# Layer 3's attention rows spread over partitions by DMA through DRAM, and a new order of work between layers 2 and 3

## What is computed

```python
def _L3_gnn_ref(X, A, Wv, bv, aw, ab, Wk, bk):
    Xw = X @ Wv + bv
    sj = Xw @ aw[:d, 0]
    si = Xw @ aw[d:, 0]
    e = leaky_relu(sj[:, None, :] + si[:, :, None] + ab[0], negative_slope=0.2)
    alpha_matrix = A * exp(e)
    transition = alpha_matrix / (sum(alpha_matrix, axis=-1, keepdims=True) + 1e-12)
    H = 0; Xk = X
    for k in range(3):
        H = H + Xk @ Wk[k] + bk[k]
        Xk = einsum('bij,bjd->bid', transition, Xk)
    return relu(H)
```

## Time and profile before

| what | value |
|---|---|
| median of 3 runs | 2437.7 us (2436.69 to 2437.82) |
| the profiled execution's own time | 2437.03 us |
| its span in the profile | 2435.1 us |
| PE matmuls busy | 2363.6 us (97%) |
| DVE, ACT, POOL busy | 1335.6, 818.1, 846.5 us (55%, 34%, 35%) |
| PE's idle time by releaser, largest | 17.3 us in 15 waits at L586, 14.4 in 2 at L303, 8.0 in 1 at L313 |

### The profile page before, as it was taken

One profiled execution on the slowest core, in us unless ns is written; L12 is line 12 of the kernel. 1 busy time (PEld: TensorE's weight loads), 2 busy tenths in 40 slices (PEclk: granted clock), 3 DMA queues, 4 the chain that ended last, 5 costly groups with the idle time before them and its releaser, 6 DMA issues.

```text
span 2435.1 us, 39821 instructions
## 1 busy us (share of the span) xinstructions
PE 2363.6 (97%) x16095; PEld 1932.4 (79%) x16095; DVE 1335.6 (55%) x2572; ACT 818.1 (34%) x1493; POOL 846.5 (35%) x1040
## 2 busy tenths in 40 slices
PE   7899999999999999999999999999789999999998
PEld 4688888888888887888888888888678888887877
DVE  2566555566556544445544455444666666665653
ACT  2344343334333333333333333333322222323221
POOL 2355445445545423233322333222441313131221
PEclk9899999999999999999999999999899999999999
DMA  5222333232333333222322223112332222223221
GB/s 169 68 81 74 88 100 92 81 85 74 82 89 107 90 111 100 57 57 71 99 58 57 57 72 98 57 57 83 102 92 72 89 73 86 77 75 88 71 72 38
DMA packets 152057, 197.98 MB, mean 81 GB/s; under 512 B 61936, under 2 KB 62016, under 8 KB 151872
## 3 DMA queue, kind: packets, MB, share of 16 engines
q1 hardware_dynamic: 151872, 195.42, 28.1%
HBM read 77.90 MB, written 50.33 MB: 53 GB/s over the span
## 4 chain that ended last, share of the span: by engine, by line
PE 71%; DVE 7%; issue 7%; POOL 6%; SPq 5%; ACT 3%; DMA 1%; ACTq 0%; DVEq 0%; POOLq 0%
PE bank L313 31%; PE bank L303 28%; SPq L1441 5%; POOL h3T_lo L1221 3%; PE bank L329 3%; PE bank L375 2%; DVE hs L665 2%; DVE stA L644 2%; ACT hn L980 1%; PE bank L522 1%; PE bank L495 1%; PE bank L293 1%; PE bank L505 1%; DVE yt L939 1%; POOL stA L1211 1%
## 5 line engine op out<-in xcount | busy, mean ns | idle before, releaser
L313 PE MATMUL bank<-w_hi,h3T_hi 128*128 128x512 f32 x768 | 304.1, 396 | 0.0
L313 PE MATMUL bank<-w_hi,h3T_lo 128*128 128x512 f32 x768 | 299.5, 390 | 0.0
L313 PE MATMUL bank<-w_lo,h3T_hi 128*128 128x512 f32 x768 | 299.5, 390 | 0.0
L633 DVE TENSOR_TENSOR Z_lo<-bank,Z_hi 128x512 fp32r<-128x512 f32 x128 | 82.9, 685 | 216.9 <-ACT Z_hi L966 216.9
L980 ACT ACTIVATE hn<-x,stA 128x512 f32<-128x512 f32 x192 | 140.7, 804 | 145.1 <-POOL stA L1213 144.1
L1208 POOL TENSOR_SCALAR stA<-stA 128x4 f32<-128x4 f32 x48 | 11.6, 242 | 485.7 <-DVE stA L646 485.6
L313 PEld LDWEIGHTS bank<-w_hi,h3T_lo 128*128 128x128 f32 x768 | 144.4, 188 | 30.4
L313 PEld LDWEIGHTS bank<-w_lo,h3T_hi 128*128 128x128 f32 x768 | 144.7, 188 | 29.8
L313 PEld LDWEIGHTS bank<-w_hi,h3T_hi 128*128 128x128 f32 x768 | 144.8, 189 | 29.5
L665 DVE STREAM_TRANSPOSE hs<-hn 128x512 f32<-128x512 f32 x192 | 123.9, 688 | 74.1 <-ACT hn L980 74.1
L633 DVE TENSOR_TENSOR cT_lo<-bank,cT_hi 128x256 fp32r<-128x256 f32 x128 | 44.8, 411 | 206.2 <-ACT cT_hi L966 206.2
(11 more groups left out here) (246 smaller groups left out, 6165.6 us busy)
## 6 DMA issues: line engine op xcount, KB each, us to landing
hGA<-hs SPq DMA_DIRECT2D x768, 64.0 KB, 2.0
mid<-x SPq DMA_DIRECT2D x32, 1024.0 KB, 4.6
x<-mid SPq DMA_DIRECT2D x32, 1024.0 KB, 5.7
x<-in_x SPq DMA_DIRECT2D x16, 1024.0 KB, 6.0
hGB<-hs SPq DMA_DIRECT2D x256, 64.0 KB, 2.0
out<-x SPq DMA_DIRECT2D x16, 1024.0 KB, 4.9
abf<-in_adj SPq DMA_DIRECT2D x64, 64.0 KB, 5.1
adj<-in_adj SPq DMA_DIRECT2D x64, 64.0 KB, 3.3
```

What stands on the lines that cost most here:

```text
L313: ins = eng.matmul(b[:], h[l][:, k, ts], W[r][:, k, :], start=(k == 0 and i == 0), stop=(last and k == 3 and i == 2))
L633: return eng.tensor_tensor(lo, src, hi.bitcast(F), ALU.subtract)
```

## The change

1. The eight `abr` tiles, their matmuls and the copies out of the banks are gone. SP writes the columns `af` to DRAM (two DMAs of 512 single elements) and reads them back as `arow`, repeated over 128 partitions.
2. The `sib` tile, its four matmuls and its bank are gone. For each group SP writes the si column to DRAM (one DMA of 512 single elements), waits for it, and reads it back as `si`, one row on all partitions (`rows3`). This stands behind the group's gather and ahead of the store of the group before.
3. In layer 3 `l3_alpha` on DVE and ACT stands behind all four z1 evictions (before: behind the third); POOL's `features_lo` stands ahead of `l3_alpha` (before: behind it).
4. Where layer 2 passes to layer 3: DVE interleaves the sums of group 0 with the VV additions; PE does both contexts ahead of the first output product and transposes group 0's adjacency there; ACT splits W3[2] and copies group 0's features ahead of the second context; group 0's alpha is taken before layer 3's loop, its row sum after the first z2 product, Thi after the second (before: after the fourth); W3[2] is split by POOL one step later.

```diff
-        ones3, bones = alloc(pc, "ones3t", [128, 128]), alloc(pc, "bones", [128, 128])
-        abr = [alloc(pc, f"abr{i}", [128, 128]) for i in range(2)]
+        si = alloc(pc, "sirows", [128, 4, 128])
+        bones = alloc(pc, "bones", [128, 128])
...
# PE
-                if prev:
+                if on and prev:
                     l2_out(g - 1, 0)
                     l2_ctx(g - 1, 1)
+                elif prev:
+                    l2_ctx(g - 1, 1)
+                    l2_out(g - 1, 0)
+                    l3_adj(0)
...
-                if g == NG - 1:
-                    for h in range(2):
-                        b, full, before = bank.take(("arow", h), (v_arow, h + 1))
...
                 for t in range(4):
                     gemm(("z2", g, t), hT3[i], t, W3[2], (v_zlo[0], 4 * g + t + 1))
                     if g == 0 and t == 0:
-                        l3_alpha(0)
-                    if g == 0 and t == 3:
                         l3_rowsum(0)
...
                     if t == 2:
-                        l3_alpha(g + 1)
+                        l3_adj(g + 1)
...
# DVE
+            def l3_alpha(g):
+                dve.wait_ge(d_si, 16 * (g + 1))
+                dve.wait_ge(v_sc, g + 1)
+                for h in HALF:
+                    eng.tensor_tensor(zc[h, :, :], si[h, :, h], scol[g % 2][h, :, 0:1].to_broadcast([64, 4, 64]),
+                                      ALU.add).then_inc(v_zc, 1)
...
+                        if g == NG - 1 and t >= 1:
+                            l3_sums(dve, eng, 0, ((0,), (1,), (2, 3))[t - 1])
...
                 for t in range(4):
                     l3_zlo(1, ("z1", g, t), g, t)
-                    if t == 2:
-                        l3_alpha(g + 1)
+                l3_alpha(g + 1)
...
# ACT
+                if not on:
+                    split_in_place(W3[2], d_w2)
+                    act.wait_ge(v_cst, 1)
+                    features2_hi(3, 0, hT3[0])
...
# POOL
-                l3_rowsource(g + 1)
-                l3_alpha(g + 1)
                 if g + 1 < NG:
                     features_lo(3, g + 1, hT3[(g + 1) % 2], hGA, p_flo3)
+                l3_alpha(g + 1)
                 l3_rowsum(g + 1)
...
# SP
+            def rows3(g):
+                if g < NG:
+                    sp.wait_ge(v_sc, g + 1)
+                    eng.dma_start(si_dr[g].rearrange("(t p) -> p t", p=128), scol[g % 2][:, :, 1], allow_slow_non_contiguous=True).then_inc(d_sc, 16)
+                    sp.wait_ge(d_sc, 16 * (g + 1))
+                    sp.wait_ge(v_zc, 2 * g)
+                    sp.wait_ge(*bank.done(("pT", NG - 1, 3)))
+                    eng.dma_start(si[:].rearrange("p t n -> p (t n)"), si_dr[g].partition_broadcast(128)).then_inc(d_si, 16)
...
+                    sp.wait_ge(v_af, 8)
+                    for h in range(2):
+                        eng.dma_start(ar_dr[h].rearrange("(k p) -> p k", p=128), af[:, :, h], allow_slow_non_contiguous=True).then_inc(d_ac, 16)
+                    sp.wait_ge(d_ac, 32)
+                    eng.dma_start(arow[:].rearrange("p h d -> p (h d)"),
+                                  ar_dr.rearrange("h d -> (h d)").partition_broadcast(128)).then_inc(d_ar, 16)
...
                 load3(g + 2)
                 gather(3, g + 1)
+                rows3(g + 1)
                 sp.wait_ge(v_x4, 4 * g + 4)
                 store_x(kA(3, g), out_v[g])
```

More of the change, by code:

```diff
@@ L81, in build @@
            for i in range(2)]
+    si_dr = [nc.dram_tensor(f"si{g}", [GT], F, kind="Internal").ap() for g in range(NG)]
+    ar_dr = nc.dram_tensor("arows", [2, D], F, kind="Internal").ap()
     mask_v = nodemask.rearrange("(g t a) n -> g a t n", g=NG, t=4)
@@ L574, in pe_program @@
                         l2_pT(g, r)
[L577 to L587, removed]
             def l3_rowsum(g):
@@ L864, in dve_program @@
                     transposes(3, 0)
-                    for h in range(2):
-                        dve.wait_ge(*bank.done(("arow", h)))
-                        eng.tensor_copy(arow[:, h, :], bank.of(("arow", h))[:]).then_inc(v_arow, 1)
                     m = dve.step(eng.tensor_tensor(sc3[:], awb[:, 0, :], awb[:, 1, :], ALU.add))
@@ L945, in l3_sums @@
         def l3_sums(dve, eng, g, ts):
-            dve.wait_ge(v_arow, 2)
-            dve.wait_ge(p_sib, g - 1)
+            dve.wait_ge(d_ar, 16)
+            dve.wait_ge(d_sc, 16 * (g - 1))
+            if g == 0:
+                dve.wait_ge(*bank.done(("qk", NG - 1, 3)))
             for t in ts:
@@ L1110, in l2_exp, with l3_alpha @@
                     eng.activation(zt[r][:], zt[r][:], ACT.Exp, scale=0.25).then_inc(a_e2, 1)
+            def l3_alpha(g):
+                if g >= NG:
+                    return
+                act.wait_ge(p_al, g - 1)
+                adj_T(3, g)
+                act.wait_ge(v_lr, g + 1)
+                eng.activation(ec3[:], ec3[:], ACT.Exp).then_inc(a_ee, 1)
             for g in range(NG + 1):
@@ L1292, in l2_residual @@
                         eng.tensor_tensor(xt[:, t, :], xt[:, t, :], bo2[:], ALU.add).then_inc(p_xb, 1)
-            def l3_rows():
-                pool.wait_ge(v_af, 8)
-                for h in range(2):
-                    for k in range(4):
-                        i = 4 * h + k
-                        if i >= 2:
-                            if i == 5:
-                                pool.wait_ge(*bank.done(("arow", 0)))
-                            else:
-                                pool.wait_ge(s_pe, {2: 1, 3: 2, 4: 3, 6: 4, 7: 5}[i])
-                        eng.tensor_tensor(abr[k % 2][:], ones3[:], af[:, k, h:h + 1].to_broadcast([128, 128]), ALU.mult).then_inc(p_row, 1)
             l2_residual(0)
@@ L1330, in pool_program @@
                         scale_A(3, 0)
[L1331 removed]
+                if g == NG - 1:
+                    eng.memset(bones[:], 0.0).then_inc(p_bones, 1)
+                    pool.wait_ge(p_bones, 1)
+                    for h in HALF:
+                        eng.memset(bones[h, h], 1.0).then_inc(p_bones, 1)
+                    pool.wait_ge(p_bones, 3)
+                    pool.wait_ge(*bank.done(("qk", g, 3)))
+                    for tl in T:
+                        for n in ("hi", "lo"):
+                            eng.memset(tl[n][:].bitcast(F), 0.0).then_inc(p_zero3, 1)
                 if g == NG:
+                    split_in_place(W3[2], "w2")
                     features_lo(3, 0, hT3[0], hGA, p_flo3)
[L1334 to L1345 removed]
             def l3_alpha(g):
@@ L1547, in sp_program @@
                     load_adj3(1)
+                    rows3(0)
                 if prev:
```

97 lines of the change are left out of this document (26 added, 71 removed).

## The result

| what | before | changed kernel |
|---|---|---|
| median | 2437.76 us (4 runs) | **2551.69 us** (4 runs, 2549.95 to 2552.93) |
| ratio | | **1.0466**, 95% interval 1.0448 to 1.0484 |
| S of group 1 | 1794.67 | 1779.79 |
| S to S, mean of groups 2 to 15 | 41.24 | 49.94 |
| last S to the end of the span | 60.1 | 70.4 |

The kernel is 114 us slower, where 34 us faster was forecast. As in the prediction, S is the moment when SP has issued a group's 16 gather DMAs. Layer 3's groups lose 13 x 8.7 us, and 5.6 from S of group 1 to S of group 2 (49.75 instead of 44.18); the tail behind the last S loses 10 us; the passage gains 15.

What follows compares the result with a forecast made beforehand. Layer 3 was taken as bound by a loop off PE, 41.24 us per group. Gains of 17 (passage) + 4 (first group) + 13 (groups) = 34 us from 2437.0 gave 2403.0, median 2404; range 2388 to 2428.

Steps and rivals of the forecast that it cites:

- the passage: From layer 2 to layer 3: the new order brings S of group 1 from 1794.67 to 1777.6, 17 us earlier.
- the store's term in x: Layer 3, each group: storing the si column to DRAM as 512 single elements lands after 2.4 us, bounds 1.2 and 5.0.
- x: Layer 3: time from S to the landing of row si, store and load in series; 5.5 us, bounds 3.7 and 10.7.
- slow store: Rival, chance 0.10: the si store's pieces set the pace, 512 cost 10 us, a group takes 47.85, time 2511.
- 256 pieces in 2.3 us: Argument against a slow si store: a 64 KB load fits 256 pieces of 256 B into its 2.3 us.
- The fit that I took from the page: Skill page's DMA costs for si's store and load: 2.0 + 2.6 + 0.2 = 4.8 us, loop 39.2, gain 22.
- The load, 2.9: Layer 3: reading si back, 256 KB on 128 partitions, lands after 2.9 us, bounds 2.3 and 5.5.
- The loop, x + 34.4 with 0.35 of disturbances: Layer 3: S to S off PE is 39.9 us, 40.25 with disturbances, instead of 41.24; gain 13 us.
- The stall at asum costs nothing: Layer 3: PE waits under 1 us for al at asum; DVE wants the following y tiles later, so no cost.
- nothing is lost behind the last S: Tail after the last group's gather issue: asum follows al or PE as before, so no change in time.
- PE's stall at si only takes up slack: Layer 3 before the change: nothing in the 40.9 us loop waits for PE, so its 1.2 us stall isn't the bound.

## Why the prediction was wrong

**The step that failed is the store's term in x**: "No row has single elements going to DRAM; I take 2.4, near the load that has the most pieces", with bounds 1.2 and 5.0. It took 8.4. Both ends of the range came from DMAs of another kind: the upper one from loads into SBUF, the lower from a 1 MB store in long pieces. A bound has to come from a row that shares the property in doubt, and here none did, so 5.0 wasn't a bound. The rival "slow store" carried 0.10 and a time of 2511; it deserved far more. Its price (16 x 0.63 from a gather DMA's issue) hit 13.1 for x by accident, since 512 pieces by themselves land in 2.0. Its time was 41 us short all the same: it had no term for the stall (1.7 in 14 groups) and none for the tail (10).

The argument "256 pieces in 2.3 us", which I set against that rival, is true and beside the point: those are long pieces that go to SBUF. The Trainium skill would have warned: "DMA: Bandwidth & Descriptors", Specifications, says that below 512 bytes a transfer is done as read-modify-write. The trace bears a price out for single elements side by side (8.4 us), and none for 16-byte pieces (1.7) or for singles 64 bytes apart (2.0), which are far below 512 bytes too; that anything is read and written back, no run here shows. The rule I did cite, that each element of a strided last dimension becomes a piece of its own, gives the right advice; the runs show that the price lay in the adjacency of the small writes far more than in their number (128 side by side 7.6 to 7.9, 512 spread 2.0). The fit that I took from the page stands there for DMAs that GpSimd issues, and these are SyncE's; its 2.0 for a store comes near the landings of spread writes, and its 4.8 for x is far from 13.0.

Step by step. A group took 49.94 instead of the forecast 40.25; of the 9.7 the store makes 6.0, the load 1.6, the stall 1.7, and some 0.4 are left over.
- *The load, 2.9.* 4.5 in the changed kernel, 3.8 with the 16-byte store, 3.4 alone. A mis-sized term: it cost 1.6. What a load of this shape takes alone (3.4) had no row either.
- *The loop, x + 34.4 with 0.35 of disturbances.* Right: with x = 13.0 it gives 47.8, and 48.2 were measured once the stall was moved. With 5.9 and the strided read it gives 41.0, measured 41.06.
- *The stall at asum costs nothing.* Right near the forecast's x (with 16-byte pieces, x = 5.9, PE waits 1 us per group and the sum holds without it), wrong at 13: PE waited 8 us, then ran at half clock (0.50 in 1991.30 to 1998.10), and y tile 3 came 1.02 late; 1.7 per group, as the version with the row sum behind all y tiles shows. That nothing is lost behind the last S was wrong too: 9 us.
- *PE's stall at si only takes up slack.* Right as far as the runs show: the version with 16-byte pieces has neither the stall nor the matmuls, and its S to S is the loop's sum with no gain from them; the version that keeps si on PE is the best.
- *The passage, 17 us.* 14.9 in the changed kernel, 13.0 to 14.5 in the versions without the row. Its steps came out near: pT's end at 1724.6 (forecast near 1725), context 1731.6 (1733.6), layer 3's first product 1752.4 (1752). The first output product came at 1735.8, 3 us before the forecast, and PE then gave it back at the adjacency transposes, which waited 3.43 for their DMA; I hadn't counted that wait. S of group 1 then came 2.2 behind the forecast, 1.6 with the transposes (their end at 1768.97, forecast 1767.4) and 0.7 with a gather of 10.79.
- *What I didn't see*: POOL's lo halves in the path of ttt. Part 3 of the change, to which I gave nothing, gained 12 us.

The best version, with the passage and the orders alone, gained 27.6 of the 34 us that were forecast, 12 of them by the part that had no term.

## What to carry over

Before a small DMA is put on the critical path, look at the shape of its writes in DRAM: 64 or more single floats side by side landed after 6 to 10 us, the same floats in pieces of 16 bytes, or spread, after 2. Make the column contiguous per partition and let the reader take the stride. And when a change has several parts, time them apart: here 28 us of gain stood behind a loss of 141.

## What the runs showed of the hardware that was not expected

- A DMA's engines can be idle (share 0.00 for 6.3 us) while its landing is not yet reported; the page's busy shares don't show that time.
- A landing of small writes goes by how densely they lie: 64 singles in 256 bytes 6.1 to 6.8 us, 512 singles 64 bytes apart 2.0.
- Such a store seems to hold up other DMAs: with the store issued 0.55 us behind it, a load of 3.4 us took 9.0 in every fourth group, and instruction packets of 16 KB took 2.9 to 3.1 us beside such stores instead of 0.9 to 1.4.
- A 16 KB instruction packet that begins during a gather goes with a gap of up to 2.8 us between two issues of SP (0.63 otherwise).
